# Strassen's product for the projection of two token groups, in phases, in an adaptive-FFN kernel on one Trainium2 core

## What is computed

```python
q_emb = relu(q @ W3 + b3)                  # q: 16 x 256, W3: 256 x 512
v_sum = sum(v, axis=1, keepdims=True)      # over the 256 tokens of a batch
h = (n * v + v_sum) * q_emb[:, None, :]    # n = 256
h = relu(h @ W2 + b2)                      # W2: 512 x 512
x_q = ternary_quantize(h, 0.33, 0.5)       # 0.5 where h > 0.33, else 0 (h >= 0)
w = ternary_quantize(weight, 0.2, 0.6) + rram_variation
out = x + einsum('bsd,od->bso', x_q, w)    # x, out: 16 x 256 x 512
```

## Time and profile before

| | us |
|---|---|
| time, median of 3 runs | 176.36 (176.15 to 176.46) |
| the profiled execution | 176.42 |
| its span, first to last instruction | 174.6 |
| TensorE busy / VectorE busy | 169.1 / 116.4 |
| ScalarE busy / GpSimd busy | 61.2 / 23.0 |

### The profile page before, as it was taken

The page is one execution under the profiler, slowest core; times in us unless marked ns, Lnnn a source line. Parts: engine busy times, 40 slices in busy tenths (PEclk is TensorE's granted clock), DMA queues, the critical chain, the costliest instruction groups (busy, mean ns, idle before and its releaser), DMA issues.

```text
span 174.6 us, 1712 instructions
## 1 busy us (share of the span) xinstructions
PE 169.1 (97%) x558; PEld 118.5 (68%) x558; DVE 116.4 (67%) x134; ACT 61.2 (35%) x161; POOL 23.0 (13%) x24
## 2 busy tenths in 40 slices
PE   7979999999999999999999999999999999999993
PEld 2859997777544478687765655767766755768883
DVE  3368999999998996785379976546183641634333
ACT  3074458693102279677104998401100000000000
POOL 3003920939002610000000000000000000000000
PEclk9999999999999999999999999999999999999999
DMA  5999999999990299995671113121853112113334
GB/s 160 263 238 237 228 218 226 221 257 301 210 204 11 69 362 244 223 343 204 178 303 60 60 60 115 41 88 60 254 226 120 42 54 90 49 73 118 122 149 151
DMA packets 31144, 28.96 MB, mean 166 GB/s; under 512 B 1536, under 2 KB 22304, under 8 KB 31136
## 3 DMA queue, kind: packets, MB, share of 16 engines
q1 hardware_dynamic: 30384, 28.33, 62.4%
q10 hardware_dynamic: 688, 0.52, 1.2%
q0 software_dynamic: 64, 0.00, 0.0%
HBM read 20.47 MB, written 8.39 MB: 165 GB/s over the span
## 4 chain that ended last, share of the span: by engine, by line
PE 88%; DVE 5%; DMA 3%; issue 1%; SPq 1%; ACT 0%; DVEq 0%; ACTq 0%
PE out_ps L704 33%; PE hid_ps L738 8%; PE hid_ps L697 6%; PE hid_ps L635 6%; PE hid_ps L642 6%; PE hid_ps L657 5%; PE hid_ps L670 5%; PE hid_ps L690 5%; PE hid_ps L678 5%; PE hid_ps L728 4%; PE hid_ps L733 4%; DMA x_in<-in_x 3%; DVE xT L374 1%; DVE wT L491 1%; DVE hid L444 1%
## 5 line engine op out<-in xcount | busy, mean ns | idle before, releaser
L704 PE MATMUL out_ps<-wT_lo,hid 128*128 128x512 f32 (+1 forms) x128 | 56.7, 444 | 0.0
L704 PE MATMUL out_ps<-wT_hi,hid 128*128 128x512 f32 (+1 forms) x128 | 49.5, 388 | 0.0
L485 DVE SCALAR_TENSOR_TENSOR x_res<-out_ps,x_res 128x512 f32<-128x512 f32 x31 | 21.3, 686 | 19.5 <-PE out_ps L704 19.5
L307 ACT ACTIVATE xT<-xT,coef,q_scale 128x256 f32<-128x256 f32 x60 | 31.1, 590 | 7.1 <-DVE coef L400 6.7
L366 DVE STREAM_TRANSPOSE xT<-x_in 128x1024 f32<-128x1024 f32 x15 | 30.8, 2056 | 1.9 <-DMA x_in<-in_x 1.8
L704 PEld LDWEIGHTS out_ps<-wT_hi,hid 128*128 128x128 f32 x128 | 24.1, 188 | 8.7 <-issue 4.3
L704 PEld LDWEIGHTS out_ps<-wT_lo,hid 128*128 128x128 f32 x128 | 24.1, 188 | 7.6 <-issue 2.2
L318 ACT ACTIVATE junk<-xT,q_emb 128x256 bf16<-128x256 f32 x40 | 19.8, 496 | 18.8 <-DVE xT L366 18.8
L738 PE MATMUL hid_ps<-xT,w_sb 128*128 128x512 f32 x32 | 13.9, 593 | 0.0
L738 PEld LDWEIGHTS hid_ps<-xT,w_sb 128*128 128x128 f32 x32 | 9.8, 310 | 3.6
L697 PE MATMUL hid_ps<-xT,s_mix 128*128 128x512 f32 x24 | 11.4, 596 | 0.2 <-DVE hid L464 0.2
(11 more groups left out here) (67 smaller groups left out, 167.6 us busy)
## 6 DMA issues: line engine op xcount, KB each, us to landing
x_res<-in_x SPq DMA_DIRECT2D x4, 2048.0 KB, 9.4
out<-x_res SPq DMA_DIRECT2D x31, 256.0 KB, 2.0
x_in<-in_x SPq DMA_DIRECT2D x24, 256.0 KB, 7.2
x_in<-in_x SPq DMA_DIRECT2D x14, 128.0 KB, 6.5
w_sb<-in_L_cond_W SPq DMA_DIRECT2D x5, 256.0 KB, 6.4
x_res<-in_L_ffn_weight SPq DMA_DIRECT2D x4, 256.0 KB, 7.0
x_res<-in_L_ffn_rram_variation SPq DMA_DIRECT2D x4, 256.0 KB, 6.4
w_sb<-in_L_cond_W ACTq DMA_DIRECT2D x1, 256.0 KB, 2.8
```

The source lines that it names most:

```text
L307: nc.scalar.activation(part, part, ACT.Identity, bias=coef[:, n, k:k + 1], scale=q_scale[:, n, k:k + 1]).then_inc(s_xs, 1)
L485: nc.vector.scalar_tensor_tensor(x_res[:, g % 2, c], out_ps[i % 4][:], SC_X, x_res[:, g % 2, c], ALU.mult, ALU.add).then_inc(s_out, 1)
L704: mm = nc.tensor.matmul(bank[:, cols], hid[:, g % 2, k, c * P:(c + 1) * P], w[:, k, cols], start=(k == 0 and w is wT_lo), stop=(k == KD - ...
```

## The change

For groups 1 and 2 the projection uses the same seven-product scheme as the hidden product. A pair of tiles (c of the first 512 tokens, c of the second 512) is the token split; hidden features and outputs are halved. GpSimd forms four sums of wT once (b_sum), ScalarE and GpSimd split them into b_hi and b_lo, and GpSimd forms four sums of the hidden values per group (a_sum, hidden_sums). Each of the seven products is 2 chunks x lo and hi = 4 matmuls of 256 columns (pair_product). Each pair uses the left half of four banks; even pairs use the banks out_ps, odd ones hid_ps. Per pair ScalarE copies P1 (copy_pair_p1), VectorE reads PSUM six times (finish_pairs), GpSimd adds three times (add_pieces).

Since hid_ps serves both, hidden products and projections no longer alternate: all hidden products of group g, then the four pairs of group g-1. Group 3's tiles are projected as before, over all eight banks. To find room in SBUF, x_in has two slots for three, x_res one buffer for two (group 3's residual is loaded into x_in), n167 is written over e1, and the new arrays share the place of w3. This moves loads: pairs from the third on wait for a later transpose, group 0's residual waits for the weight transpose, group 1's for group 0's stores. Batch 0 is loaded in eight transfers for four, and each half is transposed when it has landed. WARM_2 is 5.

The diff, cut to its core:

```diff
-    SLOTS = 3
-    WARM, WARM_2 = 8, 6
+    SLOTS = 2
+    WARM, WARM_2 = 8, 5
...
+        a_sum = sbuf("a_sum", [P, 4, 2, TOK], F32R)
+        b_hi = sbuf("b_hi", [P, 4, 2, D // 2], F32R)
+        b_lo = sbuf("b_lo", [P, 4, 2, D // 2], F32R)
+        pieces = sbuf("pieces", [P, 4, 2, D // 2])
...
+        pair_ps = [(out_ps[r][:, 0:D // 2], hid_ps[b][:, 0:D // 2]) for r, b in enumerate((1, 3, 2, 0))]
...
+            sp.wait_ge(s_tr, 1)
             load_pair(2)
             for q in range(QUADS):
                 sp.dma_start(w_in[q * BLK:(q + 1) * BLK], weight_split[q]).then_inc(s_w, DMA)
-            sp.wait_ge(s_tr, 1)
+            sp.wait_ge(s_tr, 3)
             load_pair(3)
             for q in range(QUADS):
                 sp.dma_start(r_in[q * BLK:(q + 1) * BLK], rram_split[q]).then_inc(s_r, DMA)
-            load_res(0)
-            sp.wait_ge(s_tr, 3)
+            sp.wait_ge(s_tr, 5)
             load_pair(4)
-            sp.wait_ge(s_tr, 5)
+            sp.wait_ge(s_tr, 7)
             load_pair(5)
             sp.wait_ge(s_wT, 2)
+            load_res(0)
+            sp.wait_ge(s_tr, 9)
+            load_pair(6)
+            sp.wait_ge(s_tr, 11)
+            load_pair(7)
+            store(0, range(TILES))
+            sp.wait_ge(s_stored[0], DMA * TILES)
             load_res(1)
...
+            for g in (1, 2):
+
+                pool.wait_ge(s_tsum, 4 * (g + 1))
+                hidden_sums(g)
+                for c in range(4):
+                    add_pieces(g, c)
...
+            def finish_pairs(g):
+                for c in range(4):
+                    pair_c22(g, c)
+                    pair_u2(g, c)
+                    pair_c21(g, c)
+                    pair_c11(g, c)
+                    pair_c12(g, c)
+                    pair_u3(g, c)
...
+            def pair_product(n, u, bank, hidden, weights, start, stop, tokens):
+
+                for k in range(2):
+                    for i, w in enumerate(weights):
+                        mm = nc.tensor.matmul(pair_ps[bank][u % 2], hidden[:, k, tokens], w[:, k],
+                                              start=(start and k == 0 and i == 0), stop=(stop and k == 1 and i == 1),
+                                              skip_group_check=True)
+                mm.then_inc(s_pp[n], 1)
...
+                pair_product(1, u, 0, h[:, top], block(top, left), True, False, first)
+                pe.wait_ge(s_asum, 4 * (g - 1) + 1)
+                pe.wait_ge(s_blo, 4)
...
+                pair_product(5, u, 2, a_sum[:, 0], t_sum_of(0), True, False, first)
...
+                pair_product(6, u, 1, a_sum[:, 1], t_sum_of(1), True, False, first)
...
+                pair_product(4, u, 3, h[:, bottom], t_sum_of(3), True, True, second)
+                pe.wait_ge(s_pe1, u + 1)
+                pair_product(2, u, 0, h[:, bottom], block(bottom, left), False, True, first)
+                pe.wait_ge(s_asum, 4 * g)
+                pe.wait_ge(s_o22, u + 1)
+                pair_product(3, u, 2, a_sum[:, 3], block(bottom, right), False, True, first)
+                pe.wait_ge(s_u2, u + 1)
+                pair_product(7, u, 1, a_sum[:, 2], t_sum_of(2), False, True, first)
```

More of the change, by code:

```diff
@@ L170, in adaln_ffn_kernel @@
         s_out = sem("out_tile_ready")
+        s_asum = sem("hidden_sum_ready")
+        s_bsum = sem("weight_t_sum_ready")
+        s_bhi = sem("weight_t_sum_hi_ready")
+        s_blo = sem("weight_t_sum_lo_ready")
+        s_pp = {n: sem(f"pair_product{n}_ready") for n in range(1, 8)}
+        s_pe1 = sem("pair_p1_copied")
+        s_u2 = sem("pair_p1_p6_summed")
+        s_u3 = sem("pair_p1_p6_p7_summed")
+        s_o11 = sem("pair_c11_ready")
+        s_o12 = sem("pair_p5_p3_added")
+        s_o21 = sem("pair_p4_added")
+        s_o22 = sem("pair_p5_added")
+        s_r12 = sem("pair_c12_ready")
+        s_r2 = sem("pair_c21_c22_ready")
         s_wq = sem("weight_compared")
@@ L301, in _, with scale @@
             act.wait_ge(s_q_scale, 1)
-            def scale(n):
+            def scale(n, chunks=range(KD)):
                 s, cols = slot_of(n)
-                for k in range(KD):
+                if n in SCALAR_SUMS:
+                    act.wait_ge(s_acc, KD * (SCALAR_SUMS.index(n) + 1))
+                for k in chunks:
                     part = xT[:, s, k, cols]
@@ L308, in scale, with accumulate @@
                                          scale=q_scale[:, n, k:k + 1]).then_inc(s_xs, 1)
+            def accumulate(n, chunks=range(KD)):
+                s, cols = slot_of(n)
+                for k in chunks:
+                    nc.scalar.activation(junk[:, k], xT[:, s, k, cols], ACT.Identity, scale=q_emb[:, n, k:k + 1],
+                                         accum_out=coef[:, n, k:k + 1]).then_inc(s_acc, 1)
             def scale_summed(n):
@@ L583, in _ @@
                 sum_16(g, 1)
-                finish(g - 1, 3)
+                c21(g, 0)
                 c12(g, 0)
@@ new lines, in project_pair, with block, t_sum_of @@
+            def project_pair(g, c):
+                u = 4 * (g - 1) + c
+                first, second = slice(c * P, (c + 1) * P), slice(TOK + c * P, TOK + (c + 1) * P)
+                h = hid[:, g % 2]
+                top, bottom = slice(0, 2), slice(2, 4)
+                def block(rows, cols):
+                    return wT_lo[:, rows, cols], wT_hi[:, rows, cols]
+                def t_sum_of(i):
+                    return b_lo[:, i], b_hi[:, i]
+                wait_hidden(g + 1 if c == 1 else g)
+                if u == 0:
+                    pe.wait_ge(s_out, TILES)
+                if u >= 2:
+                    pe.wait_ge(s_o11, u - 1)
+                pair_product(1, u, 0, h[:, top], block(top, left), True, False, first)
+                pe.wait_ge(s_asum, 4 * (g - 1) + 1)
+                pe.wait_ge(s_blo, 4)
+                if u >= 2:
+                    pe.wait_ge(s_o12, u - 1)
+                pair_product(5, u, 2, a_sum[:, 0], t_sum_of(0), True, False, first)
+                pe.wait_ge(s_asum, 4 * (g - 1) + 2)
+                if u >= 2:
+                    pe.wait_ge(s_u3, u - 1)
+                pair_product(6, u, 1, a_sum[:, 1], t_sum_of(1), True, False, first)
+                if u >= 2:
+                    pe.wait_ge(s_o21, u - 1)
+                pair_product(4, u, 3, h[:, bottom], t_sum_of(3), True, True, second)
[6 more added lines that the diff above has]
+                pair_product(7, u, 1, a_sum[:, 2], t_sum_of(2), False, True, first)
```

270 lines of the change are left out of this document (188 added, 82 removed).

## The result

The changed kernel takes **174.43 us**, the median of 4 runs (173.84 to 175.32), beside 176.26 us for the kernel before in the same series; the ratio is 0.988 with a 95% interval of 0.984 to 0.992. Two more series with it gave 0.986 (0.982 to 0.990) and 0.990 (0.987 to 0.993). The median of all its 14 runs is 174.35. The kernel before, whose first three runs lay within 0.3 us, has a median of 176.39 over 48 runs and spreads from 175.75 to 177.85. Four more executions, three of the kernel before and one of e8, lasted 178.7 to 179.0 us at a mean granted clock of 0.99 and are left out of every median and ratio here. Forecast was 173.7 in a range of 172.5 to 176.3: faster, as said; the time is 0.7 us above the one forecast, and the gain in this series 1.8 us for 2.7.

What follows compares the result with a forecast made beforehand. TensorE, busy 97% of the span and holding the chain of waits, was taken as the bound. 176.42 - 2.54 (Part 1) + 0.3 (Part 2) - 0.5 (Parts 3 and 4) = 173.7 us, in a range of 172.5 to 176.3.

Steps and rivals of the forecast that it cites:

- Part 1: Projection of groups 1 and 2: seven products as 224 matmuls of 256 columns at 0.120 us, saving 2.54 us.
- rival B: TensorE at edges between a pair's products: waits cost from 0.046 us per product, 178.7 us at 0.09; chance 0.11.
- rival C: Pair matmuls: the fixed 0.013 us hides in long rows, saving 5.4 us, time 170.8; chance 0.04.
- The covers: Within a pair of 3.36 us, VectorE's 2.5, GpSimd's 2.0 and ScalarE's copy of 0.51 us fit, priced at 0.
- rival D: Pairs: GpSimd's additions block VectorE's PSUM reads, 4.1 us a pair for 3.36, +6.0 us, 179.7; chance 0.03.
- Part 2: Hidden products back to back without projections between leave VectorE less time: +0.3 us, bounds 0 and 1.2.
- both tight places: Group 2's hidden phase: P7 due at T+10.30 and last P3 at T+22.32, both with zero slack.
- layout by T: Group 2's hidden phase timed from its start T = 79.85: c11 at T+6.25, sum_16's result at T+10.3.
- Parts 3 and 4: Batch 0 by halves, and two input slots with moved residual loads: together -0.5 us, bounds -1.0 and +0.8.
- the gain of the first 11 us lost again by the end of group 1: Sign of being wrong: TensorE's earlier start, taken as 0.6 us, does not last through group 1.
- Part 4: Two input slots, later load waits: under 1 us can be lost; r_in up to 2 us earlier or 0.8 later.
- rival A: Loads are late, 13.7 us at worst before; 1.0 to 2.5 us reach group 2's P7, 175.4 us; chance 0.16.

Runs made afterwards that it cites:

- e8: The kernel before with two input slots for three and both residual loads at their old places; 176.43 us, ratio 0.999.
- e6: The kernel before with all hidden products ahead of the tiles, groups 1 and 2 projected directly in halves of 256 columns; 178.66 us, ratio 1.012.
- e1: The changed kernel with batch 0 loaded whole again, by four transfers, and WARM_2 6; 174.55 us, ratio 0.988.
- e2: The kernel before with batch 0 loaded by halves and WARM_2 5; 176.59 us, ratio 1.000.
- e7_more: Second series of e5's kernel with two of batch 1's four loads issued on ScalarE's queue instead of SP's; 173.58 us, ratio 0.984.
- e4: The kernel before with two input slots and the changed kernel's order of loads, residual loads moved too; 184.77 us, ratio 1.048.
- e5: The changed kernel with the first pair's P1 ahead of the first P7 and its P4 ahead of the last P3; 173.93 us, ratio 0.985.

## Why the prediction was right, and where its terms were off

**Part 1 was right to a hundredth.** Predicted were 2.54 us saved. The four pairs of group 1 take 105.07 to 118.50 = 13.43 us, those of group 2 142.83 to 156.26 = 13.43, together 26.86 for 26.88, and 2.56 saved. TensorE's timeline at the edge of two products and at the return to hidden products answers to the earlier trace rows:

```profile
106.81 0.28 PE L921 MATMUL out_ps<-wT_lo,hid 128*128 128x256 f32 x1
...
107.17 0.28 PE L921 MATMUL out_ps<-wT_hi,hid 128*128 128x256 f32 x1
107.29 0.28 PE L921 MATMUL out_ps<-wT_lo,a_sum 128*128 128x256 f32 x1
...
118.21 0.28 PE L921 MATMUL hid_ps<-b_hi,a_sum 128*128 128x256 f32 x1
118.33 3.71 PE L819 MATMUL hid_ps<-xT,w_sb 128*128 128x512 f32 x8
```

The last product but two of a pair, P2, begins at 106.81 and P3 at 107.29: the same step of 0.12 over an edge with waits as within. That removes **rival B**, whose price began at 0.046 us per product, and **rival C**, by which the step would be 0.107.
The Trainium skill, page "TensorE: Matmul & The Clock Gate", section "Back-to-back issue gap", gives 262 cycles for 256 columns, 0.109 us at 2.4 GHz. No row agrees: 224 matmuls step at 0.120, and e6's added ones cost 0.0127 each over their columns.

The covers held as well. VectorE's six operations and GpSimd's three of a pair, GpSimd's timeline and then VectorE's:

```profile
108.55 0.74 POOL L369 TENSOR_TENSOR x_res<-x_res,pieces 128x256 f32<-128x256 f32 x1 [12.12 <-DVE x_res L653]
109.24 1.44 POOL L375 TENSOR_TENSOR x_res<-x_res,pieces 128x256 f32<-128x256 f32 x2
```

```profile
108.46 0.42 DVE L661 SCALAR_TENSOR_TENSOR pieces<-out_ps,pieces 128x256 f32<-128x256 f32 x1
109.48 0.42 DVE L626 SCALAR_TENSOR_TENSOR x_res<-hid_ps,x_res 128x256 f32<-128x256 f32 x1 [0.60 <-PE hid_ps L921]
109.90 0.42 DVE L635 SCALAR_TENSOR_TENSOR pieces<-hid_ps,pieces 128x256 f32<-128x256 f32 x1
```

VectorE reads PSUM in 0.42 us while GpSimd adds beside it, and waits for TensorE, not the reverse. **Rival D** is gone. ScalarE's copy took 0.39, GpSimd's additions 0.72 to 0.74 (0.65 was taken), the hidden sums 2.37 each. Only where the last additions meet the token sums of group 3 does anybody lose: two additions take 3.39 us there for 1.44, and token sums of 1.22 take 1.56 and 1.75. It was priced 0 with 2.5 us of slack, and P6 does not wait.

**Part 2 named both tight places and mis-sized them: +0.3 predicted, +0.86 measured.** VectorE at the start of group 2, to compare with the layout by T, answers to the earlier trace rows:

```profile
86.76 0.74 DVE L576 TENSOR_SCALAR hid<-hid_ps,th_col 128x512 fp32r<-128x512 f32 x1
87.42 2.05 DVE L496 STREAM_TRANSPOSE xT<-x_in 128x1024 f32<-128x1024 f32 x1
89.39 0.71 DVE L576 TENSOR_SCALAR hid<-hid_ps,th_col 128x512 fp32r<-128x512 f32 x1
90.02 0.74 DVE L583 SCALAR_TENSOR_TENSOR n<-hid_ps,th_col,e 128x512 f32<-128x512 f32 x1
```

TensorE's timeline has the start of the phase:

```profile
80.29 3.59 PE L819 MATMUL hid_ps<-xT,w_sb 128*128 128x512 f32 x8
```

The phase begins at T = 80.46 on the chain's scale, 0.17 us later than in the timeline, as it has 118.50 for 118.33. c11 starts at T+6.30, for T+6.25 in the layout, and sum_16 ends at 90.76 = T+10.30, to the hundredth when P7 was due. So the layout was true. But a product's weight load waits too, and it stands ahead of the product. TensorE's weight loads (PEld), an ordinary one of L858 and those of the two late products:

```profile
88.44 0.19 PEld L858 LDWEIGHTS hid_ps<-t_sum,s_mix 128*128 128x128 f32 x1 [0.24 <-issue]
...
90.88 0.30 PEld L866 LDWEIGHTS hid_ps<-t_sum,s_mix 128*128 128x128 f32 x2 [0.95 <-issue]
...
103.08 0.30 PEld L885 LDWEIGHTS hid_ps<-xT,s_mix 128*128 128x128 f32 x2 [0.64 <-DVE hid L596]
```

L858's first load begins at 88.44, 0.43 us ahead of its matmul (88.87 in the timeline), under the one ahead. The result must be there by then. P3's load waited for c22, which ended at 103.03, 0.13 us before P3's turn on the chain's scale (103.16), and still 0.19 us were lost. Zero slack to the product is 0.4 us too late for its weight load. The terms are 0.36 for the first P7 of group 2 (0.39 in this trace: 0.15 until it starts and 0.24 more in its row), 0.19 for its last P3, 0.19 for the last P3 of group 3, and 0.12 for P1 behind the short matmuls of group 1; together 0.86.
Three errors left 0.3 of these 0.86. "Group 3 has no transposes: 0" looked at VectorE's load, but this wait is not made of load: it is the chain P7, sum_167, c22, P3, with one product of 1.72 us to hide it, and it is the same length in both groups. The weight load was named, but slack was counted to the product and not to it. And the way back from a phase of 256 columns to 512 was in no row of before. The bound of 1.2 did hold it, though it had been taken from another wait, of group 1.

**Parts 3 and 4: -0.5 predicted, and what is left over can't be told from nothing.** A run's time less its first P3 of group 1 is 120.02 us in the trace of the kernel before and 118.28 to 118.30 in the changed kernel's three, so 1.73 us are gained behind that point every time, which is 2.56 - 0.86 and 0.03. The medians of the three series differ by 1.8, 2.2 and 1.6 us and the pooled ones (176.39 and 174.35) by 2.0. So 0.3 us by the pooled runs, and 0.1, 0.5 and -0.2 by the series, are left for all that happens ahead of it; e1 and e2 put the halves' own part at 0.2 and -0.2. TensorE's start was to gain 0.6 and gained 0.8 (a mean of 10.6 in the eight rows by halves, 11.4 in the first four with batch 0 whole), so the halves worked better than said there. But the step that two more issues on SP "can eat most of that" weighed them against batch 0 alone. They stand ahead of batches 1, 2 and 3 too, each of which is issued 0.9 us later, and batch 2 was the very load for which VectorE waits. So the sign "the gain of the first 11 us lost again by the end of group 1" came true on average (56.2 us on either side). Of a step that is moved, each issue must be carried to everything behind it on its queue. r_in landed once later and once earlier than before: GpSimd's sums with it start at 38.69 and 37.01 us, for 38.46. VectorE's small operation and the two scalings behind it took together 1.98 and 1.96 us for 2.74, and 2.79 in e7_more. So VectorE got 0.8 of the 1.5 us hoped for in two traces and nothing in another, and no row shows it reaching TensorE.
Part 4's slots were rightly priced at about nothing (e8). Its residual loads were right as well, by the cover named and not by the price: VectorE waits for group 0's residual, as the row says, with TensorE not waiting at all:

```profile
68.32 2.09 DVE L617 SCALAR_TENSOR_TENSOR x_res<-out_ps,x_res 128x512 f32<-128x512 f32 x3 [1.48 <-DMA x_res<-in_x]
```

68.3 us is past the limit of 68 that was set, so this sign of being wrong came true in this trace (66.7 in the two others) and cost nothing. It lands 9.0 to 9.4 us after issue each time, so **rival A** (13.7 us as at worst before) did not occur; its smaller relative, batches 1 and 2 late by more than a microsecond, did, and explains the longest of the runs. What was missed in Part 4 is group 1's residual: it was listed in the change and never priced, and e4 shows it to be a term of 8 us in the old order, held at zero by the phases. That the forecast needed no such term was luck.

**The sum with measured terms:** 176.42 - 2.56 + 0.86 = 174.7, for 174.35 measured over all runs; what lies between is the remainder above and no term of its own. Part 2 was forecast 0.6 us too low and Parts 3 and 4 some 0.2 us too low by the pooled runs, both the same way, and the range held because its bounds were wide enough for both. The interval of one series, 0.4% to either side, is also twice what had been named as the least difference that can be told.

## What to carry to other kernels

Price a shorter matmul by the pitch of its own size in the trace, not by its columns: this scheme promises an eighth and gives 9%, since every matmul has a fixed part. When work that stood between dependent products is taken out, look at each dependent chain (product, read, read, product) and count how much independent work is left beside it; count the slack to the weight load and not to the product (0.43 us earlier here), and put an independent product of the next stage into the gap (one of 0.48 us in each sufficed here). A DMA issue that is added early delays all that is queued behind it, and a buffer that is given up was free here only because a stage of other work lay between its last store and its next use.

## What the runs showed of the hardware that I had not expected

- A 256-column matmul with both kinds of float32r weights in turn costs 0.0127 us over its columns (e6: 0.81 us for 64 more). Four short ones put between two long float32 products cost 0.48 us, no more (e5); the first long products behind 112 or 128 short ones take 0.12 us more, in the changed kernel and in e6 alike.
- A float32 product whose weight load had to wait takes 1.91 to 1.96 us for 1.72, by the row of the product, beside the wait that the row shows. For the last P3 no wait is shown at all on the matmul.
- After a stall of 6.1 us TensorE came back with its granted clock at 0.50 for some 3.8 us, and the product there took 3.75 us for 1.72 (e4). The waits of up to 1.4 us ahead of the first hidden product (e1) left it at 1.00.
- VectorE's token sums beside GpSimd's additions took 1.56 to 1.75 us for 1.22, its reads of PSUM beside the same additions 0.42 as ever.
  The Trainium skill, page "SBUF — State Buffer", section "Who interferes with whom", has VectorE and GpSimd share one pair of SBUF ports under an exclusive lock. The rows agree that the two hold each other up; that it is for a whole instruction each time they do not show.
- The same loads of batches 1 and 2, in the same program, land so that VectorE starts on them 1.4 and 1.5 us apart from one execution to the next. An effect of half a microsecond at the front can't be read from one trace.
